# Counting of a sort by keys: one-hot rows of the low key bits, made by one instruction per four tiles or by one per tile

## The reference, cut to what matters

```python
edge_index = jnp.stack([src, dst])
h = jnp.maximum(_layernorm(x, axis=-1), 0.0)
x = x + _L0_gnn_ref(h, ..., edge_index, edge_type_64, 0)
...
seg_sum = jax.ops.segment_sum(e, head, num_segments=n)
w = e / seg_sum[head]
msg = w[:, None] * rel * t
summed = jax.ops.segment_sum(msg, head, num_segments=n)
```

## Time and profile before

| what | value |
|---|---|
| median of 3 runs | 10201.28 us (10199.97 to 10209.77) |
| profiled execution, device time | 10194.69 us |
| profiled execution, span | 10192.9 us |
| DVE busy over the span | 7705.4 us (76%) |
| both sorts, to the barrier behind them | about the first 1495 us |
| counting of q = 0 | 10.0 to about 171 us |
| counting of q = 1 | 750.4 to about 912 us |

### The profile page before, as it was taken

The page is one execution under the profiler, slowest core; times in us unless marked ns, Lnnn a source line. Parts: engine busy times, 40 slices in busy tenths (PEclk is TensorE's granted clock), DMA queues, the critical chain, the costliest instruction groups (busy, mean ns, idle before and its releaser), DMA issues. The chain is left out here.

```text
span 10192.9 us, 223970 instructions
## 1 busy us (share of the span) xinstructions
PE 6724.1 (66%) x64938; PEld 5458.5 (54%) x64939; DVE 7705.4 (76%) x22255; ACT 5834.0 (57%) x12496; POOL 6563.4 (64%) x5757
## 2 busy tenths in 40 slices
PE   3893986366665666656666478778878876466665
PEld 2882985254554554545555355555555533466664
DVE  9779776477776777767777699989989931677776
ACT  4224226366665666646666389979979920355543
POOL 0777750277776777767777568768858811666665
PEclk8555556578877788877888799999999988777777
DMA  0110115432222322223222212112112264222222
GB/s 23 55 45 15 60 41 197 145 52 53 53 53 44 52 53 53 52 45 52 53 53 53 49 47 59 52 47 59 52 46 59 59 209 162 47 46 46 46 46 44
DMA packets 422026, 630.49 MB, mean 62 GB/s; under 512 B 275527, under 2 KB 332321, under 8 KB 398217
## 3 DMA queue, kind: packets, MB, share of 16 engines
q0 software_dynamic: 192432, 385.10, 18.1%
q1 hardware_dynamic: 162096, 158.87, 5.0%
q10 hardware_dynamic: 67401, 85.32, 2.4%
HBM read 527.43 MB, written 103.02 MB: 62 GB/s over the span
## 5 line engine op out<-in xcount | busy, mean ns | idle before, releaser
L895 POOL DMA_INDIRECT l_land<-table,l_words x3744 | 3598.5, 961 | 1343.2 <-issue 1167.9
L1700 POOL DMA_INDIRECT ell<-gat_stage_pay,gat_stage_at x816 | 1697.1, 2080 | 248.7 <-issue 248.7
L1379 PE MATMUL left_product_ps<-k_w,messageT 128*128 128x128 f32 x5616 | 1035.2, 341 | 529.3 <-ACT messageT L1414 529.3
L1379 PEld LDWEIGHTS left_product_ps<-k_w,messageT 128*128 128x128 f32 x5616 | 872.8, 237 | 734.3 <-ACT messageT L1414 734.3
L2250 PE MATMUL rel_ps<-relation_parts,hot 128*128 128x128 bf16 x11328 | 823.6, 247 | 419.5 <-DVE hot L2349 419.5
L1797 ACT COPY gat_probT<-gat_ps 128x512 f32<-128x512 f32 (+1 forms) x2100 | 1015.3, 551 | 74.8 <-PE gat_ps L1740 66.0
L1373 PE MATMUL left_turned_ps<-ident,message 128*128 128x128 f32 x2808 | 559.1, 334 | 751.5 <-DVE message L1505 751.2
L2250 PEld LDWEIGHTS rel_ps<-relation_parts,hot 128*128 128x128 bf16 x11328 | 803.2, 114 | 441.1 <-DVE hot L2349 441.1
L244 POOL DMA_INDIRECT ell<-pay,position x816 | 841.9, 1032 | 290.4 <-issue 281.2
L1430 ACT ACTIVATE weighed<-kept,l_prob 128x128 f32 x2784 | 888.9, 391 | 59.1 <-ACT l_prob L961 58.9
L1373 PEld LDWEIGHTS left_turned_ps<-ident,message 128*128 128x128 f32 x2808 | 385.8, 173 | 853.9 <-DVE message L1505 850.7
(11 more groups left out here) (332 smaller groups left out, 15746.0 us busy)
## 6 DMA issues: line engine op xcount, KB each, us to landing
gcn_edges<-counts SPq DMA_DIRECT2D x50, 1600.0 KB, 8.1
l_land<-table,l_words POOLq DMA_INDIRECT x3744
rows<-low_dram SPq DMA_DIRECT2D x34, 1536.0 KB
counts<-pair_turned_sb ACTq DMA_DIRECT2D x12, 3200.0 KB, 9.4
logs<-pair_logs ACTq DMA_DIRECT2D x12, 3200.0 KB, 18.2
ell<-pay,position POOLq DMA_INDIRECT x816
ell<-gat_stage_pay,gat_stage_at POOLq DMA_INDIRECT x816
l_words<-ell SPq DMA_DIRECT2D x476, 8.0 KB
```

Source lines behind the costliest of these rows:

```text
L895: pool.indirect_dma_start(self.land[:, p, s, :], None, table[:, :], bass.IndirectOffsetOnAxis(ap=self.words[:, p, s, 0:1], axis=0)).then_i ...
L1379: mm = pe.matmul(right_ps[:, k * H + j, :], messageT[:, k, j, :], k_w[:, :], start=True, stop=True)
L1700: pool.indirect_dma_start(c.ells[1][:, :], bass.IndirectOffsetOnAxis(ap=stage_at[n % 2][:, t:t + 1], axis=0), stage_pay[n % 2][:, t, :], N ...
```

## The change

`hots` makes `lo_hot` with four instructions instead of one. Each takes the constant row of 128 bf16 numbers and compares it with one number per partition, a column of `lo_f`, given as a scalar operand read from memory. `hi_now`, the semaphores, the buffers and the loops are as they were.

```diff
                 def hots(h, i):
-                    V.tensor_tensor(
-                        lo_hot[:, h, :, :], spread(iota_rb[:, :], [P, H, P], 1),
-                        spread(lo_f[:, bass.ds(i * S + h * H, H)], [P, H, P], 2), ALU.is_equal)
+                    for j in range(H):
+                        V.tensor_scalar(lo_hot[:, h, j, :], iota_rb[:, :], lo_f[:, bass.ds(i * S + (h * H + j), 1)], None,
+                                        ALU.is_equal)
                     V.tensor_tensor(
                         hi_now[:, h, :, :], spread(iota_row[:, 0:NB], [P, H, NB], 1),
                         spread(hi_f[:, bass.ds(i * S + h * H, H)], [P, H, NB], 2),
```

## The result

The changed kernel takes 10235.61 us (median of 7 runs, 10228.83 to 10244.36), the kernel before 10199.87 us in the same comparison (7 runs). The ratio is 1.0036 with a 95% interval of 1.0024 to 1.0047: slower by 24 to 48 us. The forecast was 10235 us, and its total holds. The sum behind it does not: the time was lost elsewhere than the prediction put it.

A forecast was written before the change was run, and what follows sets the result against it. DVE was taken to bound counting in both sorts; 9 + 9 us for the engine and 16 for POOL's DMAs in q = 1 made 34 us on 10194.7, 10229, plus 6.6 for the median: 10235 us, range 10209 to 10272.

The forecast's parts named there:

- That DVE bounds counting, and that its delay passes one for one: Counting, both sorts: DVE fills each 0.773 us half, so its loss moves the sorts' end equally.
- The layers behind: After the sorts' barrier: nothing knows of the change, so the rest takes as long as before.
- The price of one new instruction: DVE in counting: 155 + 60 + 33 = 248 ns each, 0.162 us apart; a half 0.045 us longer.
- so I cost them at nothing: DVE's queue: three further address computations a half, 57 ns each, run ahead of the engine and add 0 us.
- the rival on the queue: DVE's queue becomes the bound in counting: 0.90 us a half, 52 us, with collisions 68, so 10269 us; chance 0.11.
- POOL's collisions, 16 us: Counting of q = 1: 110 POOL DMAs each hold DVE 0.15 us, 16 us, between 0 and 37.
- q = 0 and q = 1: The two sorts' counting: 9 us more in q = 0, 9 + 16 in q = 1 from POOL beside it.
- The sign that the prediction named: Counting: q = 1's stage longer than q = 0's, where a half takes 0.82 us; equal lengths would be wrong.
- POOL's slack: End of the sorts: POOL ends at about 1470 to 1480 us, DVE at 1525, so DVE remains later.
- And stays so: POOL in q = 1's counting: its DMAs remain slowed, 1.245 against 0.963 us each.
- The sign named for the queue: DVE in counting: idle gaps between the four `lo_hot`, put down to issue, would show the queue as bound.

The follow-up runs named there:

- `tt_two`: `lo_hot` by two two-tensor instructions of two tiles each, against the one instruction of the kernel before: 0.844 us a half in q = 0.
- `packed4`: One-hot rows interleaved by tile, all bf16, four buffers instead of two, two steps a loop pass, against the kernel before: 10108.91 us, ratio 0.9910.

## Why the prediction was right, and where it was not

- **That DVE bounds counting, and that its delay passes one for one** to the end of the sorts: right (39.6 us of the 42.3 between the spans). The layers behind were forecast as before and took 2.7 us more; in other runs on the usual chip, with the same code there, they took from 8 us less to 37 us more, so the whole time alone would not have shown this.
- **The price of one new instruction**: right. 248 ns forecast and measured, 0.162 us apart forecast and 0.163 measured, a 0.65 us row of four. `tt_two` confirms the fixed part, and the 0.06 us of the scalar from memory is the difference. With it the engine alone loses 18 us, 9 in each sort.
- **"so I cost them at nothing"**, of the further address computations: wrong, and this is the step that failed. The cover named was the 0.162 us of an instruction against 57 ns of arithmetic, but an address with its instruction holds the queue for 130 ns, and the branch, the counter and the loop's value add another 0.37 to 0.57 us in each pass, which the prediction did not count. A pass of two halves needs 1.64 us of the engine; the queue's own spacings add up to 1.63 in q = 1 and to 1.83 in q = 0. It was the rival on the queue, given 0.11 and priced at 52 us; it happened, at 19 us in q = 0 (0.916 us a half, 0.90 in the rival), of which 17.5 hang on where the loop lies in the program. In q = 1 the queue is no bound by itself; the second half's wait for PE adds about 0.01 us a half to the engine's 0.82, some 2 us.
- **POOL's collisions, 16 us**: wrong by a factor of ten, 1.6 us (0.841 against 0.833 us a half; 0.833 was found four times with POOL idle). They are there, and nearly every POOL DMA meets one, as forecast, but the lengthening of one record is not a delay of the next.
- **q = 0 and q = 1**: forecast 9 and 25 us, measured 28 and 13. The two errors, 19 too little for the queue and some 12 too much in q = 1, partly cancel, and it is luck that 34 us came so close to 36. The sign that the prediction named came out the other way round: not q = 1's counting is the longer one (173 us), but q = 0's (188 us).
- **POOL's slack**: forecast to end at 1470 to 1480 us, it ended at 1446. "And stays so", of POOL's slower DMAs in counting, was wrong: it is slowed by the two-tensor instruction and not by the four (957 ns, from 1245), and made one long pause less. That gain lies off the path.
- The sign named for the queue, idle gaps of DVE between the four, put down to issue, came in another form: 8.1 us of idle time stands in 150 us of q = 0, but ahead of the four, behind the loop's branch, and the profile puts it down to nothing.

## What to carry to other kernels

Splitting one instruction into n short ones is paid on three accounts: the engine's fixed part (here 0.07 us each), the scalar read from memory (0.06), and the queue, which needed 0.13 us for each instruction with a computed address and 0.4 to 0.6 us for a loop's end. Add up a whole pass of the loop in the queue, branch included, and hold it against the engine's time; where the two sums lie within a few per cent of each other, as here (1.64 and 1.63 us), the loop's place in the program can decide, and an edit ahead of one loop moves all loops behind it. Before taking columns faster by smaller pieces, look whether a layout lets the one large instruction run faster, and how many buffers stand between it and its reader.

## What was not expected of the hardware

- The same loop took 0.916 or 0.830 us a half depending only on how many instructions stand ahead of it: 0.12 us a pass at one place of the program and 0.08 us behind the branch. The same twenty instructions took the other sort's loop from 0.833 to 0.927 us.
- A comparison of DVE that POOL held up by 0.18 us delayed what followed by 0.02 at most.
- POOL's indirect DMAs took 1245 ns beside two-tensor instructions with both inputs f32 or mixed, and 957 ns beside the four short ones; beside the interleaved bf16 ones of `packed4` 1316 ns.
- Two chips ran the same kernel in 13.1 ms that another ran in 10.2; DVE's pace in q = 0 was equal on all three to the nanosecond. Why they differ is not shown.
